# Two graph layers on one core: distances in one fp32r pass, the adjacency product in fp32, and a new order of VectorE's turn

## The reference

```
# layer 0
h = relu(layernorm(x));  a1 = adj + I;  d = rowsum(a1) ** -0.5
x = x + relu((d * a1 * d') @ h @ W0' + b0)
# layer 1, on h = relu(layernorm(x))
c = relu(bn2(conv17(relu(bn1(h @ W1')))) + h)          # 17 taps along the nodes
s = h @ w_se' + b_se                                   # 3 numbers per node
A = exp(-(|s_n|^2 + |s_m|^2 - 2 s_n.s_m)) * adj
m = A @ relu(h @ w_msg' + b_msg)
r, z, n = GRU gates of [c, m] and h
x = x + (1 - z) * n + z * h
```

## Time and profile before

| | us |
|---|---|
| median of 3 executions | 1831.58 (1830.3 to 1832.41) |
| the profiled execution | 1831.92 |
| its span in the profile | 1830.1 |
| TensorE busy | 1790.5 |
| VectorE / ScalarE / GpSimd busy | 1188.3 / 1033.0 / 880.3 |

### The profile page before, as it was taken

How to read it: one execution, slowest core, us unless ns; L and a number is a source line. 1 busy time by engine, 2 the same in 40 slices (tenths; PEclk the granted TensorE clock), 3 DMA queues, 4 the chain that set the end, 5 groups by cost and what they waited for, 6 DMA issues and landing times.

```text
span 1830.1 us, 30613 instructions
## 1 busy us (share of the span) xinstructions
PE 1790.5 (98%) x10580; PEld 1594.4 (87%) x10580; DVE 1188.3 (65%) x2238; ACT 1033.0 (56%) x1844; POOL 880.3 (48%) x1053
## 2 busy tenths in 40 slices
PE   5999999999999999999989999999999999999998
PEld 4999999999999989999978888888888888888886
DVE  8899999899888845555765545545545545545544
ACT  5989998999898976665633323323333333333332
POOL 6788888888777736656732212212212212212211
PEclk9999999999999999999999999999999999999999
DMA  6465656566555446767873344444444344344342
GB/s 202 138 202 199 199 202 203 198 199 212 196 192 185 148 149 145 179 160 165 222 211 72 98 116 84 103 116 85 102 115 91 97 116 92 96 116 87 101 108 41
DMA packets 513816, 262.61 MB, mean 143 GB/s; under 512 B 365575, under 2 KB 473479, under 8 KB 513662
## 3 DMA queue, kind: packets, MB, share of 16 engines
q1 hardware_dynamic: 512606, 260.52, 51.9%
q10 hardware_dynamic: 1056, 0.13, 0.0%
HBM read 151.51 MB, written 109.05 MB: 142 GB/s over the span
## 4 chain that ended last, share of the span: by engine, by line
PE 95%; DVE 2%; issue 1%; ACT 1%; DMA 1%; SPq 0%; POOL 0%; ACTq 0%; DVEq 0%; POOLq 0%
PE P L113 75%; PE P L917 5%; PE P L618 4%; PE P L666 4%; PE P L645 3%; PE P L779 3%; PE P L637 2%; DVE yo L804 0%; DVE wsum L742 0%; DMA st_wg<-in_wgt 0%; DMA col<-in_cols 0%; DVE wh0l L754 0%; DVE wh2l L754 0%; ACT hd L394 0%; DVE hdxl L416 0%
## 5 line engine op out<-in xcount | busy, mean ns | idle before, releaser
L899 POOL TENSOR_TENSOR xnx1l<-xnf,xnx1h 128x1024 fp32r<-128x1024 f32 x16 | 44.3, 2768 | 342.8 <-ACT xnx1h L892 342.8
L899 POOL TENSOR_TENSOR xnx0l<-xnf,xnx0h 128x1024 fp32r<-128x1024 f32 x15 | 41.6, 2771 | 318.5 <-ACT xnx0h L892 318.5
L1000 ACT ACTIVATE tr<-P,cold 128x512 f32<-128x512 f32 x64 | 44.2, 690 | 195.0 <-PE P L113 195.0
L1003 ACT ACTIVATE nn<-gn,col 128x512 f32<-128x512 f32 x64 | 46.4, 725 | 180.4 <-DVE gn L1017 180.4
L1024 DVE SCALAR_TENSOR_TENSOR tz<-tz,tr 128x512 f32<-128x512 f32 x64 | 44.3, 692 | 148.2 <-ACT tz L1007 148.2
L548 POOL TENSOR_TENSOR axl<-af,axh 128x512 fp32r<-128x512 f32 x64 | 92.1, 1438 | 97.5 <-ACT axh L374 97.5
L1007 ACT ACTIVATE tz<-P,cold 128x512 f32<-128x512 f32 x64 | 44.1, 689 | 162.4 <-PE P L113 162.4
L1013 DVE SCALAR_TENSOR_TENSOR gn<-tr,gn 128x512 f32<-128x512 f32 x64 | 44.0, 688 | 128.0 <-ACT tr L1000 128.0
L113 PE MATMUL P<-w1mh,xxh 128*128 128x512 f32 x256 | 108.0, 422 | 0.0
L917 PEld LDWEIGHTS P<-gt,yt 128*128 128x128 f32 x768 | 98.9, 189 | 5.4 <-DMA yt<-y_d 0.5
L113 PE MATMUL P<-w1mh,xxl 128*128 128x512 f32 x256 | 101.2, 395 | 0.0
(11 more groups left out here) (202 smaller groups left out, 6831.2 us busy)
## 6 DMA issues: line engine op xcount, KB each, us to landing
xh_d<-xst SPq DMA_DIRECT2D x64, 320.0 KB, 4.7
xl<-xh_d SPq DMA_DIRECT2D x40, 512.0 KB, 6.2
y_d<-yo SPq DMA_DIRECT2D x80, 256.0 KB, 2.6
x<-in_x SPq DMA_DIRECT2D x64, 256.0 KB, 3.0
a<-in_adj SPq DMA_DIRECT2D x64, 256.0 KB, 4.4
at<-in_adjt SPq DMA_DIRECT2D x64, 256.0 KB, 4.6
x_d<-x SPq DMA_DIRECT2D x64, 256.0 KB, 4.9
xn_d<-xt SPq DMA_DIRECT2D x64, 256.0 KB, 5.0
```

Source lines behind the costliest of these rows:

```text
L899: e.e.tensor_tensor(o[1][:, :, :], xnf[p % 2][:, :, :, :].rearrange("p c i t -> p c (i t)"), o[0][:, :, :], ALU.subtract).then_inc(done, 1)
```

## The change

In the first stage:

- **Adjacency product:** `hd` and `ah` are used as they are, in fp32 (four matmuls of 256 columns), and are double-buffered. The tiles `hdx`, `ajh`, `ajl` go, with the two ScalarE copies (L321, L353), the VectorE subtraction (L416) and the GpSimd subtraction (L553) that made them.
- **Distances:** ScalarE writes the same three results as before, now to `uvf`. VectorE rounds all 96 rows to fp32r (`uvh`), then makes `uv` in two operations, where a column of 0 or -1 per row selects the high or the low part. Rows that were empty before hold copies of s, so that one fp32r product adds up high x high, low x high and high x low. The product moves from the end of turn b + 5 to the middle of turn b + 6.
- **Order:** on VectorE, L468 and L469 go behind the sum `x2` (L475); on GpSimd the scaling of `taps` goes ahead of L545. ScalarE's exp goes behind the high part of `ag`, and ScalarE takes both halves of `spectrum_out`.

Elsewhere: gate weight blocks 4 and 5 are loaded at f = 38; the first two graphs' `branch_vector` is split into both sums, then both low parts; and for the very last gate the Z sum is made in two halves of 256 columns, each with its own tanh, VectorE operations and stores.

```
 first_scalar
-            L321 copy(hdx[0], hd)          L353 copy(ajh[b % 2], ah)
-            L333 exp ahead of the relu of tcm
+            exp behind copy(ag[0], P[AG]);  spectrum_out(e, i - 7, 1)
-                e.wait_ge(S["dist"], b)
-                e.e.activation(uv[0:32, :, :], P[SXN][0:32, 0:256]...)     # and two Squares
+                e.wait_ge(S["uv"], b)
+                e.e.activation(uvf[0:32, :, :], P[SXN][0:32, 0:256]...)    # and two Squares
 first_vector
-            L416 tensor_tensor(hdx[1], hd, hdx[0], subtract);  spectrum_out(e, i - 7, 1)
+            if live(i, 6):                                   # behind xx[1], ahead of ah
+                e.wait_ge(S["uvf"], b + 1)
+                e.wait_ge(S["uv"], b)
+                e.e.tensor_scalar(uvh[0:96, :, :], uvf[0:96, :, :], 1.0, None, ALU.mult).then_inc(S["uvh"], 1)
+                e.wait_ge(S["uvh"], b + 1)
+                e.wait_ge(S["dist"], b)
+                for k, low in ((0, low_u), (1, low_v)):
+                    t = e.e.scalar_tensor_tensor(out=uv[0:96, k, :], in0=uvh[0:96, k, :], scalar=low[0:96, :],
+                                                 in1=uvf[0:96, k, :], op0=ALU.mult, op1=ALU.add)
+                t.then_inc(S["uv"], 1)
 first_gpsimd
-            L553 tensor_tensor(ajl[b % 2], ah, ajh[b % 2], subtract)
 first_tensor
-                    t = multiply(e.e, mm3([... hdx], [... (ajh, ajl)], P[AG][:, f * 256:f * 256 + 256], ...))
+                    for m in range(2):
+                        t = e.e.matmul(P[AG][:, f * 256:f * 256 + 256], hd[b % 2][:, m, f * 128:f * 128 + 128],
+                                       ah[b % 2][:, m * 256:m * 256 + 256], start=m == 0, stop=m == 1, ...)
+            if live(i, 6):        # DIST, ahead of s; was live(i, 5) at the end of the turn
 elsewhere
-        WG_LOADS = {30: 0, 31: 1, 34: 2, 36: 3}
+        WG_LOADS = {30: (0,), 31: (1,), 34: (2,), 36: (3,), 38: (4, 5)}
+            if n == 2 * NP - 1:
+                e.wait_ge(S["gn"], 2 * NP)
+                for i, k in enumerate((Z, HN)):
+                    gate(e, p, o, k, 1, [4, 5, 2, 3, 0, 1], True, True, 256 * i, 256 * i + 256).then_inc(S["gz"], 1)
+                return
```

More of the change, by code:

```diff
@@ L175, in gnn_kernel @@
         ft = p1("ft", [128, 2 * NT])
[L176 to L180, removed]
+        hd = [p1(f"hd{i}", [128, 2, 256]) for i in range(2)]
+        ah = [p1(f"ah{i}", [128, 512]) for i in range(2)]
         xs = [p1(f"x{i}", [128, 2, 256]) for i in range(5)]
@@ L210, in gnn_kernel @@
         nm = p1("nm", [128, 512])
-        uv = p1("uv", [128, 2, 256])
+        uvf = p1("uvf", [128, 2, 256])
+        uvh = p1("uvh", [128, 2, 256], F32R)
+        uv = p1("uv", [128, 2, 256], F32R)
         tcm = p1("tcm", [128, 2, 512])
@@ L639, in first_tensor @@
                 t.then_inc(S["xnt"], 1)
[L640 to L647, removed]
         def unit_parts(n):
@@ L946, in gnn_kernel, with gate @@
         HN, R, IN, Z = 0, 1, 2, 3
-        def gate(e, p, o, k, n, blocks, first, last):
+        LAST_Z = (Z, HN)
+        def gate(e, p, o, k, n, blocks, first, last, at=0, end=512):
             xc = [h[:, :, :, :].rearrange("p c i t -> p c (i t)") for h in xcx[p % 2]]
-            mov = [{**{c: xc[h][:, c, :] for c in range(2)}, **{2 + c: nmx[p % 2][h][:, c, :] for c in range(2)},
-                    **{4 + c: xnx[p % 2][h][:, c, :] for c in range(2)}} for h in range(2)]
+            mov = [{**{c: xc[h][:, c, at:end] for c in range(2)},
+                    **{2 + c: nmx[p % 2][h][:, c, at:end] for c in range(2)},
+                    **{4 + c: xnx[p % 2][h][:, c, at:end] for c in range(2)}} for h in range(2)]
             w = [{c: h[:, c, n * 256 + o * 128:n * 256 + o * 128 + 128] for c in range(6)} for h in wg]
-            return multiply(e.e, mm3(w, mov, P[k][:, :], first, last, [(c, c) for c in blocks]))
+            return multiply(e.e, mm3(w, mov, P[k][:, 0:end - at], first, last, [(c, c) for c in blocks]))
         def gates_tensor(e, p, o, middle, late):
@@ L1092, in _ @@
                     load_spectra(e, (f + 3) // 2)
-                if f in WG_LOADS:
-                    load_wg(e, WG[WG_LOADS[f]])
+                for k in WG_LOADS.get(f, ()):
+                    load_wg(e, WG[k])
                 if f == 36:
@@ L1100, in _ @@
                     freq_store(e, f, chunk)
-            for b in range(2):
+            for b in range(3):
                 load_y(e, b)
-            for k in range(4, 6):
-                load_wg(e, WG[k])
-            load_y(e, 2)
             for p in range(2):
@@ L1197, in _ @@
                 gates_scalar(e, p, 1, lambda: None, lambda: branch_scalar(e, b + 3) if more else None)
-            store_out(e, NP - 1, 1, range(2, 4))
+            store_out_half(e, 1, range(2, 4))
         @block.vector
@@ L1266, in _ @@
                 split_wg_lo(e, k)
-            branch_vector(e, 0)
-            branch_vector(e, 1)
+            for b in range(2):
+                branch_sum(e, b)
+            for b in range(2):
+                branch_lo(e, b)
             for p in range(NP):
@@ L1358 @@
     wse = np.zeros((256, 128), np.float32)
-    bse = np.zeros((128, 1), np.float32)
-    for base in (0, 32, 64):
-        wse[:, base:base + 3] = a["L1_gnn_w_se"].T
-        bse[base:base + 3, 0] = a["L1_gnn_b_se"]
+    bse = np.zeros((128, 3), np.float32)
+    for base, halves in ((0, ((0, 0), (0, -1), (-1, 0))), (32, ((0, 0), (0, -1))), (64, ((0, 0), (-1, 0)))):
+        for k, half in enumerate(halves):
+            rows_k = slice(base + 3 * k, base + 3 * k + 3)
+            wse[:, rows_k] = a["L1_gnn_w_se"].T
+            bse[rows_k, 0] = a["L1_gnn_b_se"]
+            bse[rows_k, 1:3] = half
     by_part = lambda v: v.reshape(-1, 128).T
```

163 lines of the change are left out of this document (93 added, 70 removed).

## The result

The changed kernel takes 1806.97 us (median of 4, 1805.69 to 1807.3), against 1831.1 for the kernel before on the same chip: ratio 0.9864 [0.9848, 0.9879]. The forecast was 1803.0 with a range of 1796 to 1821. The profiled execution took 1806.71 us, with a span of 1804.9 at a mean granted clock of 0.998.

What follows compares the result with a forecast made beforehand. TensorE was taken to bound the kernel, in the first stage with a gapless 10.18 us turn. Terms -21.1 - 3 + 1.3 - 4.7 - 1.2 = -28.7 from 1831.9 gave 1803.2, stated as 1803, range 1796 to 1821.

Steps and rivals of the forecast that it cites:

- The bound and the turn: First stage: TensorE stays the bound, its turn falls from 10.18 to 9.85 us, giving -21.1 us over 64 graphs.
- rival 4: Changed products in the first stage cost other than the rows say: 1844 us; chance 0.11 together with rival 2.
- The margins: First-stage turn: new operands reach TensorE in time, uv by 0.7 us, axl by 1.6, agl by 0.8.
- rival 1: Each first-stage turn: uv or agl late by 0.1 to 0.3 us, +11 us, 1815; chance 0.21.
- GpSimd holding VectorE: First-stage turn: GpSimd's powers might exclude uvh, uv and ah on VectorE; the forecast assumed they do not hold uv.
- rival 2: First stage: GpSimd's operations hold VectorE, uv 1.0 us late each turn, +57, 1860; chance 0.11 together with rival 4.
- The ramp: First turns, VectorE-bound: turns 2 to 6 each lose hdxl at 0.6 us, -3 us, between -0.5 and -5.
- The end of the first stage: Last distances come later, behind the message product, lengthening TensorE's wait for axl: +1.3 us, between 0 and +3.
- Second to third stage: Earlier load of gate weights removes TensorE's whole wait before the branch's low part: -4.7 us, at least 0.
- rival 3: Between the stages: waits stay because the branch ends last instead of the weights, 1808 us; chance 0.08.
- The tail: Behind the last product: halving the last gate's work shortens the end, -1.2 us, between 0 and -2.

Runs made afterwards that it cites:

- adj_only: Kernel before with only the adjacency product in fp32 (hd and ah double-buffered, their splits gone), distances unchanged: 1845.48 us, ratio 1.0071.
- more2: Changed kernel with two spare VectorE operations like uvh, into unread tiles, ahead of uvh in every turn: 1827.56 us, ratio 0.9974 to the kernel before.
- more3: Changed kernel with three spare VectorE operations like uvh, into unread tiles, ahead of uvh in every turn: 1852.52 us, ratio 1.0119 to the kernel before.
- tail_whole: Changed kernel with the last gate's Z sum, elementwise work and stores whole again instead of halved: 1807.81 us, ratio 0.9864 to the kernel before.
- uv_h1: Changed kernel with uvh and uv ahead of xxl on VectorE and, from turn 66, ScalarE's relu into h1 earlier: 1806.59 us, ratio 0.9861.
- drain2: uv_h1 plus four filter units before the last message product and, in the last turns, exp, uvf results and axh before h1 and xn: 1801.18 us.

## Why the prediction was right, and what it had wrong

- **The bound and the turn** (forecast 9.85 us, -21.1): right. 9.83 without a gap, and 20.5 us over 59 turns. The prices read from other rows held: 1.74 forecast and 1.73 measured for four fp32 products, 0.24 for two fp32r ones of 96 rows, so rival 4 is out. adj_only shows the first alone.
- **The margins** (0.7 us for `uv`, 0.8 for `agl`): TensorE stayed the bound and rival 1 did not come, but by less than was thought. `uv` is ready 3.89 us into the turn, as forecast (3.9); its due time was wrong. The prediction took the end of the three blocks in the chain, 4.6, while TensorE loads the weights at 4.19: 0.30 us of margin. `agl` is ready at 9.45 for a forecast of 9.0, since L547 took 1.78 and held L467 to 408.8, and is due at 9.56: 0.11 us. more2 and more3 show what lies behind the ledge. Rival 1 spoke of 0.1 to 0.3 us of lateness, and the estimates of readiness and due time together were off by 0.4 and 0.7; so that the full turns gave their -20.5 us owes something to luck.
- **GpSimd holding VectorE** (rival 2): didn't come. `uvh`, `uv` and, before, `ah` ran at their usual length beside the power. The rule of the Trainium skill ("SBUF — State Buffer", Who interferes with whom) agrees with L467 beside L547 (1.67 us in place of 0.68). Beside the power of 1.01 us on 128x4 the trace does not show it: `uv`, with two SBUF inputs, took 0.88 there, and 0.87 at 646.76, where GpSimd was idle.
- **The ramp** (-3): -2.5, inside the bounds, but the working fits only in part. 1.9 of it is there before the first product (12.18 for 14.06), where a cast and the low part are gone; the prediction had counted 0.6 in each of five turns. adj_only shows 3.2 for the removed splits alone. In the changed kernel the granted clock took some back: its window of 20 to 40 us stands at 0.91, and the output products there took 1.3 us longer than the same twelve in tail_whole, whose first stage is identical:

```profile
29.96 2.90 PE P L113 x12
```
```profile
30.27 1.64 PE P L113 x12
```

  In five profiles with this same first stage turn 7 starts between 44.59 and 47.55 us, so a ramp read from one profile is good to some 1.5 us.
- **The end of the first stage** (+1.3, between 0 and +3): this is the step that was mis-sized; it is +7.3. The working counted one wait, that for the last `axl`, from the place of the last distances alone, and that wait came as forecast: 3.1 us for 1.8 + 1.3. The others were not in it. In the traces, idle time from turn 66 to the last message product went from 1.8 to 7.65 us in seven pieces, 0.46 at 630.0 the first; the work between is 0.2 less; and the slow clock behind the last wait took 1.65. The prediction checked the deadlines of a full turn of 9.85 us and took them to hold where turns are 7 to 8.7 us. The experiments take back 5.5 of it.
- **Second to third stage** (-4.7): the wait went as forecast, so rival 3 is out, but the gain is 7.4. The rows for the rest were there: 7.20 us for 18 products, 3.1 more than at full clock. The slow clock behind a wait goes with the wait. The Trainium skill ("TensorE: Matmul & The Clock Gate", HAM oscillation — how this bites in real kernels) tells of TensorE falling to half its clock when it waits for data; here the trace agrees, 0.50 after 4.7 us.
- **The tail** (-1.2): -2.3 by the trace, less 0.2 for the narrower products. The four VectorE operations were sized well (2.36 for 2.3); that the stores end 1.0 us earlier was not counted.

The sum came out at -25.2 us of span for -28.7: 6.0 lost in the drain and 1.1 in turns and ramp, 3.6 more gained between the stages and at the tail. The forecast is right in its main mechanism, TensorE's turn. Its distance of 4 us from the measured time is a difference of errors that partly cancel, and that is luck.

## What to carry to other kernels

A pipeline's deadlines must be checked twice: at the length of a full turn, and where steps fall away and turns get shorter, since a chain through all engines that hides in the full turn sets the pace there. Read when an operand of TensorE is due, and whether TensorE waits for it, from the rows of the weight loads: the end of the block in front came 0.38 us later here, and more2's chain showed 0.02 us idle where the weight load showed 0.42. Price a wait of TensorE of some us with the slow products that may follow it (1.65 to 3.1 us behind waits of 2.5 to 4.7 here), not with its own length alone, and look for work that is due anyway to put into it. When removing one of two chains that bind at the same place, name the other one first: uv_h1 moved 4 us of waits from one to the other and gained none.

## What the runs showed of the hardware that was not expected

- TensorE began to load the weights of the distances at 404.88, 0.38 us before the block in front of them ended; an operand that came later than that delayed the turn by as much (more2: 0.34 us late, +0.30 a turn), although TensorE's product rows show almost no idle time.
- The granted clock was 0.50 behind a wait of 4.7 us, and 0.66 on the mean of the 4 us behind one of 3.1; the products there cost 3.1 and 1.65 us extra. drain2's waits of up to 1.45 us left it at 1.00. In the ramp, behind waits of 1.9, 1.5 and 1.0 us, the window of 28 to 32 us stands at 0.73 in the profile of the changed kernel and at 0.59 in that of its repeat, but at 1.00 in more3 and adj_only, which have waits of nearly the same lengths there. What decides this is not shown.
- GpSimd's product of 128x512 held a VectorE sum with two SBUF inputs for 1.0 us, and itself took 1.78 us in place of 1.28; its power of 128x4, 1.01 us long, held none of the VectorE operations beside it in the turns shown.
